# Flamingo stack on one core: landing waits at each fourth table gather, query spreads ahead of the last eight, five products on constants ahead of the first turned rows

## The reference

```python
x = x + tanh(g[0]) * experts(layernorm(x), ctx)        # layer 0: 8 experts, 2 of them for a token
x = x + tanh(g[1]) * quantised_mlp(layernorm(x))       # layer 1
x = x + tanh(g[2]) * block_attention(layernorm(x), ctx)# layer 2: 16 heads
x = x + tanh(g[3]) * pick_of_8(layernorm(x))           # layer 3
x = x + tanh(g[4]) * mlstm(layernorm(x), ctx, hops)    # layer 4
# in mlstm, for 8 heads of 16 channels:
pos_emb = rpe[hops]                                    # 128 x 128 rows of 128 numbers out of a table of 2017
k_hop   = einsum('bhvc,vmhc->bhvm', q, pos_emb)        # added to the scores q.k
x = ...                                                # layers 5, 6 and 7: experts by capacity, slots, ternary mlp
```

## Time and profile before

| | |
|---|---|
| median of 3 runs | 742.83 us (742.33 to 744.86) |
| profiled execution | 744.14 us, of which 742.3 us lie between its first and last instruction |
| PE busy | 650.9 us (88%), granted clock 0.953 of full in the mean |
| DVE, ACT, POOL busy | 575.5, 514.9, 336.5 us |
| table gathers (line 1523) | 128, of 1033 ns in the mean |

### The profile page before, as it was taken

The page is one execution under the profiler, slowest core; times in us unless marked ns, Lnnn a source line. Parts: engine busy times, 40 slices in busy tenths (PEclk is TensorE's granted clock), DMA queues, the critical chain, the costliest instruction groups (busy, mean ns, idle before and its releaser), DMA issues.

```text
span 742.3 us, 13812 instructions
## 1 busy us (share of the span) xinstructions
PE 650.9 (88%) x5039; PEld 447.9 (60%) x5039; DVE 575.5 (78%) x1134; ACT 514.9 (69%) x1062; POOL 336.5 (45%) x346
## 2 busy tenths in 40 slices
PE   5278999588898998998999999988999999999857
PEld 5157887233454554655995666556888676666612
DVE  5869996887899857998665888669883347778887
ACT  4875762566887764677538776758885688888676
POOL 4777675776777777889000000169970040000000
PEclk7589999899999999999899999989999999999998
DMA  8526582111111114410000000700000000000001
GB/s 302 182 56 184 132 133 76 51 46 40 34 34 34 34 52 78 65 44 8 1 1 1 0 1 1 285 3 1 2 1 1 1 1 1 1 0 1 1 0 57
DMA packets 40274, 36.11 MB, mean 49 GB/s; under 512 B 21801, under 2 KB 30257, under 8 KB 40209
## 3 DMA queue, kind: packets, MB, share of 16 engines
q1 hardware_dynamic: 33616, 21.73, 10.0%
q0 software_dynamic: 6592, 13.51, 8.1%
HBM read 30.11 MB, written 5.11 MB: 47 GB/s over the span
## 4 chain that ended last, share of the span: by engine, by line
PE 58%; DVE 20%; ACT 9%; issue 4%; POOL 4%; DMA 4%; SPq 0%; ACTq 0%; DVEq 0%; POOLq 0%
PE ps L1357 5%; PE ps L1597 4%; PE ps L2375 3%; PE ps L1634 3%; POOL pe L403 3%; PE ps L2111 3%; PE ps L2062 3%; PE ps L1625 3%; PE ps L1005 3%; PE ps L213 2%; PE ps L1615 2%; DMA pe<-normed_rows,pe 2%; PE ps L1542 2%; PE ps L1034 2%; PE ps L2341 2%
## 5 line engine op out<-in xcount | busy, mean ns | idle before, releaser
L1523 POOL DMA_INDIRECT pe<-in_rpe,idx x128 | 132.3, 1033 | 35.6 <-issue 24.8
L384 POOL DMA_INDIRECT pe<-normed_rows,pe x46 | 49.1, 1068 | 18.5 <-issue 9.4
L1999 POOL TENSOR_SCALAR big<-big,wcols 128x256 f32<-128x256 f32 x1 | 1.4, 1429 | 121.2 <-DMA big<-in_l3f_w 121.2
L528 ACT ACTIVATE pe<-ps,wcols 128x256 f32<-128x256 f32 x92 | 38.6, 477 | 21.8 <-PE ps L435 21.7
L1740 ACT ACTIVATE big<-ps,small 128x128 f32<-128x128 f32 x128 | 34.8, 383 | 17.4 <-PE ps L1625 17.4
L1357 PE MATMUL ps<-nT,big 128*128 128x512 f16 x192 | 44.4, 379 | 0.0
L1215 ACT ACTIVATE big<-ps 128x1024 f32<-128x1024 f32 x32 | 32.7, 1020 | 15.4 <-PE ps L1002 15.2
L2375 PEld LDWEIGHTS ps<-big,pe 128*128 128x128 f32 x288 | 34.7, 192 | 8.4 <-issue 5.3
L435 PE MATMUL ps<-big 128*128 128x256 f16 x276 | 35.3, 279 | 5.1 <-DVE big L579 4.2
L1235 DVE TENSOR_REDUCE small<-ps 128x16 f32<-128x1024 f32 x32 | 38.2, 1215 | 1.0 <-PE ps L996 1.0
L403 POOL DMA_INDIRECT pe<-tile_results,pe x32 | 30.8, 962 | 13.7 <-issue 7.3
(11 more groups left out here) (432 smaller groups left out, 1977.4 us busy)
## 6 DMA issues: line engine op xcount, KB each, us to landing
pe<-in_l2f_w SPq DMA_DIRECT2D x16, 256.0 KB, 6.6
tile_results<-big SPq DMA_DIRECT2D x23, 128.0 KB
pe<-in_xrow SPq DMA_DIRECT2D x4, 512.0 KB, 5.1
big<-in_l0x_w SPq DMA_DIRECT2D x8, 256.0 KB, 6.8
pe<-in_rpe,idx POOLq DMA_INDIRECT x128
cT<-in_cT SPq DMA_DIRECT2D x2, 512.0 KB, 4.7
nT<-in_l0x_w SPq DMA_DIRECT2D x4, 256.0 KB, 8.0
vx<-in_l0x_w SPq DMA_DIRECT2D x4, 256.0 KB, 9.3
```

What stands on the lines that cost most here:

```text
L384: pool.indirect_dma_start(out=xg16[:, i % RX, h, :, :].rearrange("p r n -> p (r n)"), out_offset=None, in_=xrows_d, in_offset=bass.Indirec ...
L528: ins_ = act.activation(hid32[:, i % RF, f, :], hidden_ps(i, u)[:, f % 2, :], ACT.Relu, bias=wcols[:, bass.ds(at + (COL_AT["l0x_b1"][0] + ...
L1523: pool.indirect_dma_start(out=pe[:, v * D:(v + 1) * D], out_offset=None, in_=ins["rpe"], in_offset=bass.IndirectOffsetOnAxis(ap=idx[:, v:v ...
```

## The change

1. The table gathers outside layer 2's loop lose their pauses (those between the gathers of tile results, line 403, stay). In their place `pool_landed` waits, ahead of each fourth gather, until all gathers so far have landed (from v = 20 on).
2. Layer 2's loop on POOL has a 16th step, so it issues v up to 87 rather than 84, and steps 14, 15 and 16, which write no query block, wait for PE's place in the loop, as the earlier ones do in `pool_queries`.
3. `pool_rest4` moves from behind all gathers to ahead of v = 120.
4. PE does five products of `ones` with `ones` (128 by 512, f32) into bank 6, which nothing reads before tile 0's results overwrite it: two ahead of the register read, three ahead of the first turned rows.

```diff
--- before.py
+++ after.py
@@ -387,8 +387,8 @@
                     pool.memset(pause[:, 0:1], 0.0).then_inc(s_set, 1)
                     pool.wait_ge(s_set, POOL_FIRST)
             for v in range(EARLY, IN_L0):
-                if v % 2 == 0:
-                    pool_pause(pool, link)
+                if v > EARLY and v % VG == 0:
+                    pool_landed(pool, v // VG - 1)
                 pool_gather(pool, v)
             for k in range(RY):
                 pool.wait_ge(s_ys[k], 16 * len(range(k, NT, RY)))
@@ -470,6 +470,10 @@
             for t in range(BC):
                 mm = te.matmul(bank(c)[:, t * D:(t + 1) * D], combT[:, tok(c * BC + t)], l0x_b2[:], start=True, stop=True)
             mm.then_inc(R0["pe_step"], 1)
+
+        def pe_fill(te, n):
+            for _ in range(n):
+                te.matmul(bank(6), ones[:], ones[:].unsqueeze(1).to_broadcast([128, 4, 128]), start=True, stop=True)
 
         def pe_layer0(te):
             te.wait_ge(s_set, 1)
@@ -496,8 +500,10 @@
                     te.wait_ge(R0["act_step"], ACT_ROW + k - (PICKS * B - ACT_ROWS) + 1)
                 mm = te.matmul(bank(2)[:, 0:NG], row_of[:, k, :], tile_of[:, k, 0:NG], start=(k == 0), stop=(k == PICKS * B - 1))
             mm.then_inc(R0["pe_step"], 1)
+            pe_fill(te, 2)
             te.wait_ge(R0["dve_step"], DVE_TILES)
             ats = tile_numbers(mybir.EngineType.PE, eid_pe, 4 * F * (E - 1))
+            pe_fill(te, 3)
             pe_turn_rows(te, 0)
             for i in range(NT + 2):
                 if i < NT:
@@ -1171,19 +1177,21 @@
         def pool_layer2(pool, link):
             pool_queries(pool, 0)
             for v in range(IN_L0, IN_L0 + 8):
-                if v % 2 == 0:
-                    pool_pause(pool, link)
+                if v % VG == 0:
+                    pool_landed(pool, v // VG - 1)
                 pool_gather(pool, v)
             pool.wait_ge(R0["dve_step"], DVE_ROWS + 2 * NCH)
             pool_queries(pool, 1)
             pool_queries(pool, 2)
             for v in range(IN_L0 + 8, IN_L1):
-                if v % 2 == 0:
-                    pool_pause(pool, link)
+                if v % VG == 0:
+                    pool_landed(pool, v // VG - 1)
                 pool_gather(pool, v)
-            for b in range(1, B):
+            for b in range(1, B + 1):
                 if b + 2 < B:
                     pool_queries(pool, b + 2)
+                else:
+                    pool.wait_ge(A2["st"], 2 * (b + 2 - QS) + 2)
                 for v in range(IN_L1 + PER_STEP * (b - 1), IN_L1 + PER_STEP * b):
                     if v >= KEYS_AT and (v - KEYS_AT) % VG == 0 and v < 64:
                         pool.wait_ge(A2["s"], 2 * ((v - KEYS_AT) // VG) + 2)
@@ -1192,9 +1200,11 @@
                     pool_gather(pool, v)
                 if b in KEYS_IN:
                     pool_keys(pool, POOL_KEYS[KEYS_IN.index(b)])
-            for v in range(IN_L1 + PER_STEP * (B - 1), S):
-                if v % 2 == 0:
-                    pool_pause(pool, link)
+            for v in range(IN_L1 + PER_STEP * B, S):
+                if v % VG == 0:
+                    pool_landed(pool, v // VG - 1)
+                if v == REST_AT:
+                    pool_rest4(pool)
                 pool_gather(pool, v)
 
         def act_queries(act, c):
@@ -1514,6 +1524,7 @@
         PER_STEP = 3
         IN_L0 = EARLY + 12
         IN_L1 = IN_L0 + 12
+        REST_AT = S - 2 * VG
         qhalf = big[:, 0:QR * NH2 // 2 * S].rearrange("p (r n) -> p r n", r=QR)
 
         def pool_gather(pool, v):
@@ -1522,6 +1533,9 @@
                 pool.wait_ge(s_pos[g % 2], 16 * VG * (g // 2))
             pool.indirect_dma_start(out=pe[:, v * D:(v + 1) * D], out_offset=None, in_=ins["rpe"],
                                     in_offset=bass.IndirectOffsetOnAxis(ap=idx[:, v:v + 1], axis=0)).then_inc(s_pos[g % 2], 16)
+
+        def pool_landed(pool, g):
+            pool.wait_ge(s_pos[g % 2], 16 * VG * (g // 2 + 1))
 
         def pool_pause(pool, link):
             link(pool.memset(pause[:], 0.0))
@@ -2674,8 +2688,6 @@
                 pool_layer4(pool, link)
             if stop > 2:
                 pool_layer2(pool, link)
-            if stop > 4:
-                pool_rest4(pool)
             if stop > 5:
                 pool_layer5(pool, link)
             if stop > 6:
```

## The result

The changed kernel takes **746.95 us** (22 runs, 743.42 to 750.91), the kernel before 744.35 us in the same table (22 runs, 742.05 to 747.31). The ratio is 1.0036, 95% interval 1.0023 to 1.0050: 2.6 us slower, where I forecast no difference that can be told. The number is close to that of my rival "the last groups are late" (747.3), but in part by luck: that rival stood on a baseline of 743.0, and the kernel before measures 744.35 over 22 runs. Counted as a change, the rival said 4.3 us and the forecast 0.2; measured are 2.6.

The account below looks back on a forecast made before the run. PE was taken to lead (58% of the chain), POOL mattering only where somebody waits for it. Terms 0.2 + 0 + 0 + 0 on the profiled 744.14 gave 744.3, hence a median of 743.0 us, range 741.0 to 745.8.

Parts of the forecast that it names:

- the last groups are late: Rival: PE waits for the last table groups at its last turns, 4.3 us late, 747.3 us; chance 0.07.
- The five products: Layer 0's start: tile 0's turns 1.5 us late, 1.27 regained by an earlier clock rise; 0.2 us taken as cost.
- Landing waits after the tiles: Two waits, 4 and 1.2 us, less 1.2 for pauses; gathers end at 120.6, ahead of 121.17; cost nothing.
- Tile results late: Rival: the first landing wait after the tiles at its worst costs 2.3 us, 745.1 us; chance 0.04.
- Layer 2's start and the step waits: At layer 2's start 0.3 us is absorbed by POOL's idle 2.65; steps 14 to 16 delay only POOL's gathers; nothing.
- The last stretch: POOL's final table gathers and `pool_rest4`: `pool_rest4` starts at 337.3, group 31 lands at 369.4 before its turn; cost 0.
- Eight landing waits of 1.2: For v = 88 to 119, eight waits of 1.2 us each, bringing these gathers to 57 us in all.
- DVE's hindrance: `pool_rest4` meets DVE's second burst of six spreads and takes 3.6 us more, ending at 357.
- the hand: Time between group 31 landing at 369.4 and PE turning it at 374.08: 4.7 us.
- My bound of 11: Upper bound, in us, of time in hand at group 31 if each `pool_rest4` operation takes 1.16 us.
- the low clock that may fall away: Rival: PE's low clock around 345 disappears, 2 to 3 us less, 740.5 us; chance 0.11.
- The DVE lock: Rival: `pool_rest4` makes DVE's two bursts wait 1.45 us each, 2.9 in all, 745.7 us; chance 0.07.

Follow-up runs that it names:

- e1: Kernel before with only the five products added: 745.62 us, ratio 1.0016.
- e2: Changed kernel without the five products: 744.93 us, ratio 1.0008.
- e11: Changed kernel without products and with `pool_rest4` behind all gathers: 745.34 us, ratio 1.0006.
- e10: As e11, with pauses among the tile result gathers replaced by a landing wait ahead of each 8: 749.89 us, ratio 1.0064.
- e17: Changed kernel without the five products, as e2, on a chip where the kernel before takes 862.32 us: 790.26 us, ratio 0.9167.
- e18: Changed kernel as it is, on a chip where the kernel before takes 862.32 us: 791.25 us, ratio 0.9165.
- e5: Kernel before plus the waits of steps 14 to 16, landing waits from v = 88 and `pool_rest4` ahead of v = 120: 807.06 against 873.92 us, ratio 0.9238.
- e3: Changed kernel with `pool_rest4` back behind all gathers: 746.55 us, ratio 1.0025.
- e4: Changed kernel with pauses instead of landing waits in the last stretch, from v = 88 on: 746.07 us, ratio 1.0011.
- e6: Kernel before with landing waits in place of pauses up to v = 39 only: 864.38 against 873.92 us, ratio 0.9892.
- e9: Changed kernel run again as it is, on a chip where the kernel before takes about 744 us: 747.25 us, ratio 1.0025.

## Why the prediction was wrong

- **The five products**: right in every number of e1's trace (35.1, 37.7, 1.47, then hidden). In the changed kernel's own the clock rose at 36.6 and the turns began at 38.44, still inside the bounds, and PE's waits for rows (1.85 and 1.18) took it up. On the mean the products stay unsettled: 1.0016 with an interval that holds both nothing and 2.7 us, 0.9997 on another chip, and the four kernels with them and the early waits came out 1.1 to 3.6 per mille above before, the two with the waits and without them 0.8 and 0.6. That the products cost something beside the early waits is therefore a rival that no run rules out.
- **Landing waits after the tiles**: mis-sized. I took 1.2 + 4 for the two waits beyond the usual 0.30 each; measured 6.6 (5.47 + 1.69 less 0.60). With the products (four kernels) the two waits hold 7.0 to 8.1 us of idle time, without them (e2, e11, e10) 6.5 to 6.7; I had summed the two edits apart. Why they differ is not shown: the row gathers ahead of them stand only 0.1 later against the work around. The next gather moved from "120.6, ahead of 121.17" to 122.73. "Tile results late" was a rival of 0.04 at 2.3 us and came true for some 1.1.
- **Layer 2's start and the step waits**: nothing, as forecast. v = 88 started at 284.63, 4.3 behind the forecast, and 3.9 of this is the shift of the whole execution by then.
- **The last stretch is the step that failed.** "Eight landing waits of 1.2": measured 2.25 us of idle on the mean in place of 0.30, so 1.95 each, 6.0 more in all. I took 2.44 less 1.25 and left out the step from the landing to the next gather's start (0.25 in the chain of the changed kernel, 372.61 to 372.86), so even an undisturbed wait adds 1.5 (1.77 less 0.30), and beside DVE's work up to 2.8. Slower gathers, and 0.4 at the start, made up the rest of a start of `pool_rest4` that is 7.2 late (348.42 less 3.9, against 337.3). My 3.6 for DVE's hindrance did not come (15.88 for 16.04), which gave half of it back. The wait ahead of group 31, also taken as 1.2, then held 3.72 us of idle time, because group 30 landed late. Group 31 landed at 379.08, or 375.2 without the shift of 3.9, where I had 369.4: 5.8 late against 4.7 in hand. In the kernels where group 30 landed as usual and the clock was low at 345, the hand was 1.3 to 1.4 (e2, e17, e18). My bound of 11 for it was wrong as well: by the sum's own terms it is 15 (337.3, 9.3 and 12.4, against 374.08).
- **The hand was counted against one execution.** PE's 374.08 contains a low clock at 345 that is not always there. Without it PE is 1.7 us earlier, and 5.8 - 4.7 + 1.7 is 2.8 of the 2.9 us lost. Both executions of the changed kernel on 744 chips without it lost 2.9 us; those of e2, e17 and e18 that had it lost nothing. In e5, on an 870 chip with the clock full there, no products and an ordinary landing of group 30 (1.80 us idle ahead of group 31), PE waited 1.01 us for group 31 and turn 31 came 9.4 us behind turn 29 in place of 8.24, so 1.2 were lost. I had both pieces, the low clock that may fall away and the late groups, and held them for two rivals, one of them fast. They are one: without the low clock its gain is mostly taken back, and with a slow landing of group 30 another us goes too. That the instruction packet beside group 30 makes its landing slow is argued from two traces; no run moved it.
- **The sum** by what the traces show: some 1.1 at the tile results in both traced executions of the changed kernel on 744 chips, and 2.9 at groups 30 and 31 in both. In how many of the other executions PE waits there isn't known. If it is half, the sum is 2.6, as measured, but that half is my assumption, and so this division is argued, not shown. The lateness at the results, read from one execution each, is near the time over before of e3 (1.2 against 1.9), e4 (0.9 against 0.8), e2 and e11 (0.5 and 0.6 against 0.6 and 0.4), and further off in e1 (0.1 against 1.2), each within its interval.
- **The DVE lock** is no cause: `pool_rest4` took 15.88 us where it took 16.04, although DVE's second burst now met it, and the six spreads of a burst took 1.89 us in place of 1.80. But "POOL gave way and DVE did not" holds for this place only. Where POOL's eight spreads stand behind the gathers and DVE has only two of its own at a time, POOL's take 10.01 us and DVE's two up to 1.88 (e3) for 0.72 before:

```profile
361.36 1.88 DVE L1441 TENSOR_SCALAR big<-nT,consts 128x256 f32<-128x256 f32 x2
```

```profile
359.68 0.72 DVE L1433 TENSOR_SCALAR big<-nT,consts 128x256 f32<-128x256 f32 x2
```

The Trainium skill ("SBUF — State Buffer", "Who interferes with whom") says that one engine waits for the other's whole instruction. The traces agree for both engines: POOL's 4.98 us in the changed kernel, beside DVE's long row of spreads, and DVE's 1.16 more in e3, which is one whole operation of POOL (1.17). DVE's loss did not reach PE, whose turns 29 to 31 take the same 8.24 us in e3; POOL's is in the 15.88 above.

## What to carry to other kernels

A wait for landing costs a gather's latency and the step to the next gather, less the usual distance (1.5 us here), and more beside a busy VectorE. Count what is left in hand at the last consumer against a run in which everything else goes well, since a low clock that hides a delay in one execution is gone in the next. Edits that each fit into a cover may share it: here the kernels with both the products and the early waits were later at the tile results than those with one of them, though the runs do not show how. A change that costs a little on one chip may take 8% off on another, so it pays to run it on more than one before dropping it.

The version to keep is therefore not the changed kernel but its landing waits alone (e11: 1.0006 on a 744 chip), with `pool_rest4` behind the gathers and no products. On an 870 chip it was run only with waits at each eighth (0.9266); all but the products was run as it is (0.9167).

## What the runs showed of the hardware

On three of five chips this program took 16 to 17% longer, and its instruction loads came late beside GpSimd's stream of small gathers: none between 313 and 388 us in e6, with PE, DVE and ACT idle for up to 51 us at a time, until some 5 us behind the stream's end. A wait for landing at each fourth gather, or each eighth, lets the loads through (0.9167, 0.9266); a memset of 0.22 us between gathers does not. In the traces from the other two chips the loads pass amid the same stream. There the touch is smaller and the other way round: beside a 16 KB instruction packet the last of a gather's 16 parts landed 1.9 us (changed kernel) and 1.2 us (e9) behind the other 15. Whether the cause is the chip, or who else uses its queues, no run here tells.
